# Selective-scan layers: 64x64 quadrants for the injected term, and another order of ScalarE's copies

## The reference, cut to what matters

```python
for i in range(DEPTH):                       # 4 layers
    xi, z = split(x @ in_w[i].T)             # 256 channels each
    u  = silu(causal_conv(xi, conv_w[i]) + conv_b[i])
    dt, B, C = split(u @ xp_w[i].T)          # 8, 16, 16 columns
    delta = softplus(dt @ dt_w[i].T + dt_b[i])
    # for each channel d and state s, over t:
    # h[t] = exp(delta[t] * A[d, s]) * h[t-1] + delta[t] * u[t] * B[t, s]
    # y[t] = sum_s h[t] * C[t, s] + u[t] * D[d]
    x = (y * silu(z)) @ out_w[i].T
```

## Time and profile before

| | before |
|---|---|
| median of 3 runs | 1195.49 us (1194.45 to 1196.18) |
| the profiled execution | 1195.5 us, span 1193.8 us |
| busy: PE, PEld | 1026.2 us (86%), 529.2 us (44%) |
| busy: DVE | 943.2 us (79%) |
| busy: POOL | 802.9 us (67%) |
| busy: ACT | 781.3 us (65%) |
| DMA queues | 117.5 MB, 31.3% of 16 engines |

### The profile page before, as it was taken

The page is one execution under the profiler, slowest core; times in us unless marked ns, Lnnn a source line. Parts: engine busy times, 40 slices in busy tenths (PEclk is TensorE's granted clock), DMA queues, the critical chain, the costliest instruction groups (busy, mean ns, idle before and its releaser), DMA issues. The chain is left out here.

```text
span 1193.8 us, 21258 instructions
## 1 busy us (share of the span) xinstructions
PE 1026.2 (86%) x7673; PEld 529.2 (44%) x7673; DVE 943.2 (79%) x1737; ACT 781.3 (65%) x1722; POOL 802.9 (67%) x449
## 2 busy tenths in 40 slices
PE   5799999999899999999999999883485799999465
PEld 2344444444444444444444444341254466666244
DVE  3578888888988889888898898996795346664895
ACT  4868888787787878878878778851242145554342
POOL 1488988879798798898997988993343023322252
PEclk8899998999999999999999999997687579999688
DMA  6544334435344435444444343403600100000001
GB/s 231 168 153 127 146 122 143 125 115 169 109 148 129 135 124 164 123 141 127 143 132 138 124 144 127 146 32 81 99 1 0 18 19 17 5 19 2 0 1 36
DMA packets 65403, 118.89 MB, mean 100 GB/s; under 512 B 40004, under 2 KB 46980, under 8 KB 56324
## 3 DMA queue, kind: packets, MB, share of 16 engines
q1 hardware_dynamic: 65300, 117.54, 31.3%
HBM read 109.13 MB, written 6.29 MB: 97 GB/s over the span
## 5 line engine op out<-in xcount | busy, mean ns | idle before, releaser
L838 POOL TENSOR_TENSOR prod<-hid,c_rep 128x1024 f32<-128x1024 f32 x256 | 605.0, 2391 | 117.1 <-DVE hid L774 117.1
L774 DVE TENSOR_TENSOR_SCAN hid<-decay,acc 128x256 f32<-128x256 f32 x1024 | 606.7, 662 | 69.2 <-PE acc L497 67.2
L676 ACT ACTIVATE decay<-delta,a_neg 128x255 f32<-128x255 f32 x1024 | 423.3, 497 | 14.3 <-DVE hid L774 14.1
L497 PE MATMUL acc<-b_diag,du_t 64*128 64x256 f32 x2048 | 294.3, 407 | 24.2 <-DVE hid L774 24.2
L497 PEld LDWEIGHTS acc<-b_diag,du_t 64*128 64x128 f32 x2048 | 179.0, 188 | 201.7 <-issue 116.6
L511 PE MATMUL ring<-prod,ident 64*64 64x512 f32 x2048 | 261.9, 629 | 4.1 <-POOL prod L838 3.4
L1663 POOL TENSOR_SCALAR_AFFINE_SELECT att_probs<-att_probs 128x512 f32<-128x512 f32 x64 | 40.6, 634 | 133.5 <-ACT att_probs L1707 133.5
L511 PEld LDWEIGHTS ring<-prod,ident 64*64 64x64 f32 x2048 | 68.7, 138 | 126.9 <-issue 118.7
L1707 ACT ACTIVATE att_probs<-acc 128x384 f32<-128x384 f32 x128 | 55.8, 488 | 79.1 <-PE acc L1474 79.1
L414 PE MATMUL ring<-xpad,diag_cw 64*64 64x512 f32 x512 | 62.1, 601 | 0.9 <-ACT xpad L593 0.9
L1472 PE MATMUL acc<-att_qk 17*128 17x256 f32 x256 | 56.7, 461 | 0.5 <-ACT att_probs L1707 0.4
(11 more groups left out here) (165 smaller groups left out, 1374.1 us busy)
## 6 DMA issues: line engine op xcount, KB each, us to landing
c_rep<-c_rows SPq DMA_DIRECT2D x64, 1024.0 KB, 4.8
b_diag<-diag_rows SPq DMA_DIRECT2D x64, 512.0 KB, 3.8
diag_rows<-prod SPq DMA_DIRECT2D x2, 2048.0 KB, 10.8
att_qk<-in_pos_q SPq DMA_DIRECT2D x4, 768.0 KB
att_qk<-att_dense SPq DMA_DIRECT2D x32, 64.0 KB
att_qk<-in_pos_k SPq DMA_DIRECT2D x4, 288.0 KB
resid<-in_x SPq DMA_DIRECT2D x4, 256.0 KB, 3.1
c_rows<-bc SPq DMA_DIRECT2D x64, 8.0 KB, 1.4
```

What stands on the lines that cost most here:

```text
L497: last = nc.tensor.matmul(inj[:, K % 2, at:at + HALF * SG], du_t[rows, n % 2, e, q * INNER + h * P:q * INNER + (h + 1) * P], b_diag[rows, ...
L676: last = nc.scalar.activation(decay[:, K % DECAYS, s, 1:], delta[:, n % 2, h, e * SEQ + 1:(e + 1) * SEQ], ACT.Exp, scale=a_neg[:, lay(n) % ...
L774: last = nc.vector.tensor_tensor_scan(hid[:, K % HIDS, s, :], decay[:, K % DECAYS, s, :], rows[:, s, :], 0.0, ALU.mult, ALU.add)
L838: nc.gpsimd.tensor_tensor(prod[:, K // 4 % 2, h, :, at], hid[:, K % HIDS, :, :], c_rep[:, g, :, at], ALU.mult).then_inc(s_prod, 1)
```

## The change

It does three things. In `inject`, each matmul of 64 rows by 128 columns becomes two of 64 by 64, on the two halves of the channels (m); the number of matmuls and weight loads of the injection doubles, the length of each (256) stays. On TensorE, dut moves from k = 9 to 10 and both xi products stand at k = 11. On ScalarE, `read_xp` moves in front of the decays of k = 3; `silu_u` and `silu_gate` move from k = 0 to 1; `softplus` stays at 6 but without `read_bt` ahead of it, which goes to 7; `read_out` 7 to 8, `read_z` 8 to 9, `read_dut` 10 to 11, `read_xi` 11 to 12. On GpSimd `times_u` moves from k = 8 to 7.

```diff
@@ inject
-                            last = nc.tensor.matmul(inj[:, K % 2, at:at + HALF * SG], du_t[rows, n % 2, e, q * INNER + h * P:q * INNER + (h + 1) * P],
-                                                    b_diag[rows, K // 4 % 2, e * 2 + q, :], start=True, stop=True)
+                            for m in range(2):
+                                chans = q * INNER + h * P + m * HALF
+                                last = nc.tensor.matmul(inj[m * HALF:(m + 1) * HALF, K % 2, at:at + HALF * SG],
+                                                        du_t[rows, n % 2, e, chans:chans + HALF], b_diag[rows, K // 4 % 2, e * 2 + q, :],
+                                                        start=True, stop=True)
@@ tensor, loop over k
-                            if k == 9:
+                            if k == 10:
                                 dut(n + 1)
-                        if n + 2 < NPAIR and k in (10, 11):
-                            xi(n + 2, k - 10)
+                        if n + 2 < NPAIR and k == 11:
+                            xi(n + 2, 0)
+                            xi(n + 2, 1)
@@ scalar, loop over k
+                        if k == 3 and n + 1 < NPAIR:
+                            read_xp(n + 1)
                         decays(K + 3)
-                        if k == 0:
+                        if k == 1:
                             if n + 1 < NPAIR:
                                 silu_u(n + 1)
                             silu_gate(n)
                             nc.scalar.preload_act_table_set(EXP_LOG)
                         if n + 1 < NPAIR:
-                            if k == 3:
-                                read_xp(n + 1)
                             if k == 4:
                                 read_dt(n + 1)
                             if k == 6:
+                                softplus(n + 1)
+                            if k == 7:
                                 read_bt(n + 1)
-                                softplus(n + 1)
-                            if k == 8:
+                            if k == 9:
                                 read_z(n + 1)
-                            if k == 10:
+                            if k == 11:
                                 read_dut(n + 1)
                             if k == 13:
                                 scale_skip(n + 1)
-                        if k == 7 and n and not last_layer(n - 1):
+                        if k == 8 and n and not last_layer(n - 1):
                             read_out(n - 1)
-                        if k == 11 and n + 2 < NPAIR:
+                        if k == 12 and n + 2 < NPAIR:
                             read_xi(n + 2)
@@ gpsimd, loop over k
-                        if k == 8 and n + 1 < NPAIR:
+                        if k == 7 and n + 1 < NPAIR:
                             times_u(p, nc.gpsimd, n + 1)
```

## The result

The changed kernel takes 1162.6 us (median of 4 runs, 1154.2 to 1167.1) against 1195.5 (1194.5 to 1196.2): ratio 0.972, 95% interval 0.965 to 0.978. That is 33 us faster, inside the range, and 14 us slower than the 1149 that was forecast. The four runs lie 13 us apart, and the mean granted clock goes the other way, 0.913, 0.908, 0.899 and 0.898 for 1154.2, 1158.3, 1167.0 and 1167.1 us. The runs of the kernel before here lie 2 us apart, but six more of it beside the experiments lie between 1185.8 and 1200.6 us, at clocks from 0.927 to 0.914: such a spread is not new.

What follows compares the result with a forecast made beforehand. A chain of hand-overs between PE and ACT, closing once per pair, bounds the kernel: 32.6 + 12.3 + 0.3 = 45.2 us instead of 48.3; over 15 pairs 46 us off 1195.5 gives 1149 us, range 1137 to 1180.

Steps and rivals of the forecast that it cites:

- The borders between shapes: On PE, quadrants remove the cost of switching tile shape: injection 0.865 instead of 1.06 us, addition 1.72 instead of 1.88.
- the sequencer: On PE, some 62 ns per matmul would add some 1.5 us a pair; the forecast took no such cost.
- rivals, 2 and 3: In the injection: 2, borders not of shape, 1194 us, chance 0.06; 3, loads don't hide, 1284 to 1314 us, 0.07.
- The loop: Scan stage, once per pair: ACT from xp's end 12.3 us, then PE from out to xp 32.6, sum 44.9.
- The 0.3 us that were added for phases: Per pair, an allowance for phases between DVE and POOL, raising the loop from 44.9 to 45.2 us.
- This is what is late next.: PE at out waits for the ring bank that the later b_t copy empties, perhaps 1.7 us, where it had no wait.
- rival 1: A new wait closes a longer loop through out, clamp, softplus and injection: 1164 to 1182 us, chance 0.15.
- That is this pair's period; the mean is 1.4 above it.: Kernel before: chain of 46.9 us; the mean is longer because DVE also waits for softplus's logarithm, 16.0 us in all.
- The reorder alone is worth nothing.: Reordering without any gain from quadrants leaves the loop at 48.2 us a pair, 1194 us, no change.
- DVE's waits for the injection: Sign in the scan stage: DVE's waits for PE's injection fall from 54.1 us to under half.
- Softplus, du, SP.: DVE's stall for the logarithm goes; dut and times_u moves cost nothing; SP's stores cost nothing, with two blocks of margin.
- has almost no slack: POOL (GpSimd), busy 43.5 us a pair, has almost no slack at a 45.2 us period; given in support of rival 1.

Runs made afterwards that it cites:

- the filled wait: Changed kernel with 8 added 64x64 products of zeros put into PE's wait at out, no wait removed: 1141.8 us, ratio 0.957.
- The best kernels: The four kernels at ratios 0.948 to 0.950 to the kernel before, which can't be told apart: 1132.7 to 1137.3 us.
- order only: Changed kernel with the old injection of 64 rows by 128 columns put back: 1184.2 us, ratio 0.991.
- again: The changed kernel as it is, measured again beside the kernel whose wait at out is filled with work: 1163.1 us, ratio 0.974.
- quadrants only: Kernel before with only the injection split into 64x64 products, no reordering: 1183.7 us, ratio 0.991.
- filled at dt: Kernel before with the 64x64 injection alone, plus two added 128x128 products ahead of each dt on PE: 1169.4 us, ratio 0.975.
- two moves: Kernel before with the 64x64 injection, SiLU and gate at k = 1, and xp's copy ahead of the decays of k = 3: 1147.7 us, ratio 0.960.
- dut later: The two-moves kernel with dut at k = 10, both xi at 11, read_dut 11, read_xi 12, times_u 7: 1137.3 us, ratio 0.948.
- b_t behind softplus: Changed kernel with the b_t copy directly behind softplus on ACT, at k = 6 instead of 7: 1133.7 us, ratio 0.948.
- out read at k = 7: Changed kernel with the b_t copy ahead of softplus at k = 6, and read_out at k = 7 instead of 8: 1135.2 us, ratio 0.950.
- b_t ahead of softplus: Changed kernel with the b_t copy ahead of softplus at k = 6, as the kernel before had it: 1132.7 us, ratio 0.948.

## Why the prediction was right or wrong

- **The borders between shapes.** Right: 0.86 and 1.72 us, block 2.58 instead of 2.94, as worked out. Neither the loads in quadrants nor the sequencer cost anything there. Of the rivals, 2 and 3 are out by these rows.
- **The loop.** Right in place and size: 44.9 us by the sum, 44.7 in every pair whose clock holds; with the old injection 47.9 by the sum, 47.8 measured. With its weakest link, the b_t copy, one block earlier, pairs at full clock went from 44.7 to 44.0 us, so the copy stands in the loop. The 0.3 us that were added for phases did not show.
- **"This is what is late next."** The wait at out was foreseen at 1.7 us and is 2.26. It had its place in the sum as time. What the sum lacked is what idle time does to PE: in 8 of 14 pairs of one profiled execution, and in all of another, out and its neighbours ran at 1.2 GHz behind it, and a pair became 46.1 to 47.7 us instead of 44.7. This term was set to nothing, without a reason; by the filled wait it is worth 1163.1 - 1141.8 = 21 us. In its shape it is rival 1 (a new wait closes a longer loop; 1164 to 1182 us), but not by that rival's mechanism: clamp and softplus wait no longer than expected.
- **"That is this pair's period; the mean is 1.4 above it."** The cause named, DVE's wait for the logarithm, is right but not the first in the row. Seven of the nine such waits of about 1.5 us or more follow a stretch of half clock behind PE's wait at dt, as this one does:

```profile
397.94 1.13 PE L454 MATMUL ring<-bc,wd 8*128 8x256 f32 x8 [1.30 <-ACT bc L621]
400.34 3.31 PE L511 MATMUL ring<-prod,ident 64*64 64x512 f32 x16
406.91 0.28 ACT L630 ACTIVATE b_t<-ring 128x32 f32<-128x32 f32 x2 [3.00 <-PE ring L443]
409.35 1.96 DVE L766 TENSOR_TENSOR delta<-delta,soft 128x1024 f32<-128x1024 f32 x1 [1.57 <-ACT soft L645]
```

  The additions take 3.31 instead of 1.95 us, so the bt product, its copy, softplus and DVE are late. The term that the sum left out was thus already in the kernel before. The moves took the wait at dt away and opened another at out.
- **"The reorder alone is worth nothing."** Wrong: 11 us, of which 15 x 0.4 were in the sum of the loop, and 5.6 in the first pair, which I had priced like the others; and it keeps the clock up, which had no term. "Quadrants" and "order" were priced as if their gains added up from the first one; in fact 12 and 11 us alone make 33 together. Without ScalarE's moves PE turns its gain into idle time ahead of dt.
- **DVE's waits for the injection** were to fall under half of 54.1 us; they are 46.6. The sign was set too low by the prediction's own numbers: each block of 2.58 us is still longer than the 2.3 us that DVE's four scans take, so there are 136 small waits instead of 77 larger ones; part is the slow clock (longest 3.3 us).
- **Softplus, du, SP.** As said: no wait of DVE for the logarithm, none of PE for du, no late transfer.

That 1162.6 came within 14 us of 1149 is in part luck. With the clock held the pairs take 44.7 us, not 45.2, and the kernel 1141.8, 7 us below the forecast; the clock adds 21. The median lies between the forecast's own band (1138 to 1162) and rival 1's (1164 to 1182).

The best kernels stand at 44.0 us a pair because GpSimd is busy 43.7 of them, as far as the trace tells. The prediction's remark that GpSimd "has almost no slack" is right for them, and not yet for the changed kernel, where it waits 21 us for DVE between 60 and 720 us.

## What to carry to other kernels

Price a new wait on the matmul engine twice: as time on the chain, and as idle time after which the matmuls may run at half clock. To tell the two apart, put harmless matmuls into the wait; if the kernel gets faster by added work, the wait should go or be filled. And when two engines hand over to each other once per turn, sum the loop from rows in order of time before pricing each edit: neither engine's gain counts until the other is early enough. When shortening the loop gives less than its sum says, look for an engine that is busy for the whole of a steady turn.

## What the runs showed of the hardware that was not expected

- PE idle for 2.27 us ahead of out: out's four instructions take 3.78 instead of 1.98 us, the injection behind it 1.99 instead of 1.09. The same idle time in another pair has no such effect (1.98 us). Idle times of 1.74 and 1.03 us close together (order only) were followed by it in one pair of 14, and a single one of 1.3 us at dt in six pairs of the kernel before. So the length of an idle time alone doesn't say whether the clock falls; what else decides stays open.
- Stretches of half clock between 80 and 700 us of the profiled executions: before 6, changed 7 and (again) 13, quadrants only 10, filled at dt 3, two moves 4, dut later 5, b_t behind softplus 2, out read at k = 7 4; none in order only, filled at out, and b_t ahead of softplus.
- The kernel's spread follows: 1154 to 1167 us at mean clocks from 0.913 to 0.898, and 1139.9 to 1143.9 at 0.929 to 0.926 with the wait filled.
- Sixteen 64x64 matmuls of 256 elements, with sixteen weight loads, stream in 0.86 us, 27 ns for each of the 32 instructions. The weight loads of the injection at 408.73:

```profile
408.31 0.15 PEld L499 LDWEIGHTS acc<-b_diag,du_t 64*64 64x64 f32 x4 [0.28 <-issue]
408.74 0.58 PEld L499 LDWEIGHTS acc<-b_diag,du_t 64*64 64x64 f32 x12 [0.28 <-issue]
```

  Four loads stand ahead of it and twelve beside its own matmuls, which run in all four quadrants. By the Trainium skill (TensorE: Matmul & The Clock Gate, "Wait — 56ns, not 53.3ns?") a matmul takes some 62 ns of the sequencer where hardware decoding is off; these rows show 54 ns a matmul and no such bound, and no run shows which way of decoding was on. The same page of the Trainium skill, in its part "Packing small matmuls", says in one sentence that a weight load overlaps a matmul in flight only where the row group differs, and in another that loads into a background weight buffer are pulled ahead too. The rows here contradict the first and would fit the second.
